# Loading each expert's weights once, in 256 KB pieces split where they land, in a sorted expert MLP kernel

## The reference, cut to what matters

```python
Wi_b, Wo_b = Wi[expert_idx], Wo[expert_idx]            # 512 x 2048 and 2048 x 512 per token
h = gelu(einsum('bsh,bhi->bsi', x, Wi_b) + bi_b)       # 128 x 2048
o = einsum('bsi,bih->bsh', h, Wo_b) + bo_b             # 128 x 512
r = o + x
y = (r - mean(r)) * rsqrt(var(r) + 1e-12) * gamma_b + beta_b
out = rotate(y, theta, phi)
```

## Time and profile before

| | before |
|---|---|
| median of three runs | 2757.75 us (2749.0 to 2760.32) |
| the profiled execution | 2766.84 us, span 2765.0 us |
| TensorE matmul, busy | 2677.4 us (97%) |
| VectorE busy | 1956.6 us (71%) |
| GpSimd busy | 1319.9 us (48%) |
| ScalarE busy | 936.3 us (34%) |
| DMA, mean | 136 GB/s |

### The profile page before, as it was taken

How to read it: one execution, slowest core, us unless ns; L and a number is a source line. 1 busy time by engine, 2 the same in 40 slices (tenths; PEclk the granted TensorE clock), 3 DMA queues, 4 the chain that set the end, 5 groups by cost and what they waited for, 6 DMA issues and landing times.

```text
span 2765.0 us, 54858 instructions
## 1 busy us (share of the span) xinstructions
PE 2677.4 (97%) x12310; PEld 1208.9 (44%) x12311; DVE 1956.6 (71%) x4931; ACT 936.3 (34%) x1697; POOL 1319.9 (48%) x1560
## 2 busy tenths in 40 slices
PE   5999999999999999999999999999999999999998
PEld 2444444444444444444444444444444444444443
DVE  5677777676777776776777776767767776677776
ACT  6333333333333333333333333333333333333332
POOL 0687447860037870677500577607873677500000
PEclk9999999999999999999999999999999999999999
DMA  6766655855455855668644658646665657444343
GB/s 187 187 152 153 154 149 129 182 136 103 87 133 135 184 133 114 170 122 178 140 91 90 159 120 184 144 92 167 166 157 128 172 121 179 111 97 87 83 96 65
DMA packets 741351, 375.98 MB, mean 136 GB/s; under 512 B 682816, under 2 KB 682944, under 8 KB 732608
## 3 DMA queue, kind: packets, MB, share of 16 engines
q1 hardware_dynamic: 677136, 173.16, 35.9%
q0 software_dynamic: 27312, 135.28, 15.2%
q10 hardware_dynamic: 36864, 67.13, 7.9%
HBM read 174.13 MB, written 33.55 MB: 75 GB/s over the span
## 4 chain that ended last, share of the span: by engine, by line
PE 81%; DMA 6%; DVE 5%; issue 4%; DVEq 2%; ACT 2%; ACTq 0%; SPq 0%; POOLq 0%; POOL 0%
PE z_ps L833 41%; PE o_ps L842 40%; DMA xT<-x 3%; DMA xbuf<-in_x 2%; DVE z_ps L641 1%; DMA hT<-h 1%; DVEq L197 1%; ACT z_ps L444 1%; DVE h L651 0%; ACT x L439 0%; DMA wi<-in_L_cond_Wi 0%; ACTq L197 0%; DVE y L696 0%; DVE ln L668 0%; DVE r_ps L667 0%
## 5 line engine op out<-in xcount | busy, mean ns | idle before, releaser
L833 PE MATMUL z_ps<-wi,xT 128*128 x6096 | 1406.5, 381 | 32.3 <-issue 16.1
L842 PE MATMUL o_ps<-wo,hT 128*128 (+1 forms) x6144 | 1410.7, 379 | 10.8 <-DMA hT<-h 10.8
L833 PEld LDWEIGHTS z_ps<-wi,xT 128*128 128x128 f16 x6096 | 598.0, 98 | 763.1 <-issue 61.2
L842 PEld LDWEIGHTS o_ps<-wo,hT 128*128 128x128 f16 x6144 | 601.8, 98 | 739.8 <-issue 19.8
L444 ACT ACTIVATE z_ps<-z_ps 128x512 f32<-128x512 f32 x512 | 299.5, 585 | 1732.3 <-DVE z_ps L641 1727.9
L641 DVE SCALAR_TENSOR_TENSOR z_ps<-z_ps,tok,bi_all 128x512 f32<-128x512 f32 x512 | 387.2, 757 | 195.2 <-PE z_ps L833 133.1
L378 POOL TENSOR_TENSOR wi<-staged 128x512 f32<-128x512 f32 x112 | 118.5, 1058 | 658.1 <-DVE r_ps L661 647.0
L651 DVE SCALAR_TENSOR_TENSOR h<-z_ps,tok,h 128x512 f16<-128x512 f32 x512 | 380.2, 743 | 10.0 <-ACT h L450 9.5
L450 ACT ACTIVATE h<-z_ps,tok 128x512 f16<-128x512 f32 x512 | 351.9, 687 | 19.0
L646 DVE SCALAR_TENSOR_TENSOR x<-xbuf,tok,x 128x512 f16<-128x512 f16 (+1 forms) x128 | 117.2, 916 | 185.8 <-ACT x L439 185.8
L696 DVE SCALAR_TENSOR_TENSOR y<-r_ps,rot,y 128x128 f32<-128x128 f32 x512 | 194.5, 454 | 5.2 <-ACT y L457 2.0
(11 more groups left out here) (126 smaller groups left out, 1366.9 us busy)
## 6 DMA issues: line engine op xcount, KB each, us to landing
staged<-in_L_cond_Wi POOLq DMA_DIRECT2D x56, 1024.0 KB, 5.9
staged<-in_L_cond_Wo POOLq DMA_DIRECT2D x56, 1024.0 KB, 6.6
xbuf<-in_x ACTq DMA_DIRECT2D x128, 256.0 KB, 3.3
out<-y ACTq DMA_DIRECT2D x128, 256.0 KB, 3.4
hT<-h SPq DMA_TRANSPOSE x512, 4.1
bi_all<-in_L_cond_bi POOLq DMA_DIRECT2D x7, 1024.0 KB, 8.3
wi<-in_L_cond_Wi SPq DMA_DIRECT2D x4, 1024.0 KB, 8.5
wo<-in_L_cond_Wo POOLq DMA_DIRECT2D x4, 1024.0 KB, 5.9
```

The lines of the kernel that those rows point to most:

```text
L833: last = t.matmul(z_ps[:, n, :], xT16[:, j, a, k, :], wi16[:, bass.ds(b, 1), w, k, cs], start=(k == 0 and (a, w) == PASSES[0]), stop=(k == ...
L842: last = t.matmul(o_ps[:, j, :], hT16[:, n, a, c, :], wo16[:, bass.ds(b, 1), w, n * GC + c, :], start=(n == 0 and c == 0 and (a, w) == PAS ...
```

## The change

Each expert's weights are loaded once, in 32 pieces of 128 x 512 float32 (256 KB) instead of 16 loads of 1 MB. A piece lands in the place of its own two halves: `wi16` and `wo16` are laid out by piece (`[P, 2, NC, 2, BANK]` with NC = 16 pieces, high half beside low half), so that the 2 KB of a piece in each partition are exactly the float32 piece before the split. `staged` is gone; three small buffers hold a scaled piece, a squared piece and the sum.

Nothing of a rank is loaded ahead of the wait on `s_res` any more. After it, four pieces are issued one behind the other; then each of the 16 steps of Wi waits for its piece, squares it, adds it to the sum and issues the piece four ahead. After every second step comes an eighth of the bias (`bi_piece`, 128 KB). While the 16 pieces of Wi are split, the first 12 steps also wait for a piece of Wo and issue the one four ahead. bo, gamma and beta come one by one in steps 0, 4 and 8 of Wo (256 KB each, `bgb_piece`). The fold starts at 256 columns in place of 1024. The split scales the piece into `scaled`, copies it to the high half and subtracts for the low half. The matmuls read the same 512 columns from new addresses; rank 0 writes its halves through `half_of`.

```diff
-        wi16 = sb("wi16", [P, 2, 2, KH, I], F16)
-        wo16 = sb("wo16", [P, 2, 2, KI, H], F16)
-        staged = sb("staged", [P, 2, QN])
+        wi16 = sb("wi16", [P, 2, NC, 2, BANK], F16)
+        wo16 = sb("wo16", [P, 2, NC, 2, BANK], F16)
+        scaled = sb("scaled", [P, BANK])
+        squared = sb("squared", [P, BANK])
+        summed = sb("summed", [P, BANK])
...
+        def bi_piece(queue, e, b, j, landed):
+            c = slice(j * BIP, (j + 1) * BIP)
+            queue.dma_start(bi_all[:, b, c], bi[bass.ds(e, 1), c].broadcast_to([P, BIP])).then_inc(landed, 16)
+
+        def bgb_piece(queue, e, b, j, landed):
+            v = (bo, gamma, beta)[j]
+            queue.dma_start(bgb_all[:, b, j, :], v[bass.ds(e, 1), :].broadcast_to([P, H])).then_inc(landed, 16)
...
             def split(hi, lo, raw, scale):
-                chain.step(g.tensor_scalar(hi, raw, scale, 1.0, ALU.mult, ALU.mult))
-                chain.step(g.tensor_scalar(raw, raw, scale, 1.0, ALU.mult, ALU.mult))
-                chain.step(g.tensor_tensor(lo, raw, hi, ALU.subtract))
+                chain.step(g.tensor_scalar(scaled[:], raw, scale, 1.0, ALU.mult, ALU.mult))
+                chain.step(g.tensor_copy(hi, scaled[:]))
+                chain.step(g.tensor_tensor(lo, scaled[:], hi, ALU.subtract))
...
-                stage(0)
-                stage(1)
...
+                def load(j):
+                    m, c = divmod(j, NC)
+                    k, n = divmod(c, NB)
                     if m == 0:
+                        source = Wi[bass.ds(e, 1), k * P:(k + 1) * P, n * BANK:(n + 1) * BANK]
                     else:
+                        source = Wo[bass.ds(e, 1), c * P:(c + 1) * P, :]
+                    pool.dma_start(raw(m, c), source.rearrange("e p n -> p (e n)")).then_inc(s_stage[j % 4], 16)
...
+                if not boot:
+                    pool.wait_ge(s_res, before)
+                for j in range(4):
+                    load(j)
+                for c in range(NC):
+                    landed(c)
+                    sum_squares(0, c)
+                    load(c + 4)
+                    if c % 2:
+                        bi_piece(pool, e, b, c // 2, s_bias[b])
+                matrix_scale(0)
+                bias_scale()
+                for c in range(NC):
+                    halves(0, c)
+                    if c < NC - 4:
+                        landed(NC + c)
+                        load(NC + c + 4)
+                g.engine_nop().then_inc(s_wi, 1)
+                if not boot:
+                    pool.wait_ge(s_ln, before)
+                for c in range(NC):
+                    if c >= NC - 4:
+                        landed(NC + c)
+                    sum_squares(1, c)
+                    if c % 4 == 0 and c < 12:
+                        bgb_piece(pool, e, b, c // 4, s_bgb[b])
+                matrix_scale(1)
+                for c in range(NC):
+                    halves(1, c)
+                pool.wait_ge(s_bgb[b], (r + 1) // 2 * 48)
+                g.engine_nop().then_inc(s_wo, 1)
...
-                        last = t.matmul(z_ps[:, n, :], xT16[:, j, a, k, :], wi16[:, bass.ds(b, 1), w, k, cs],
+                        last = t.matmul(z_ps[:, n, :], xT16[:, j, a, k, :], wi16[:, bass.ds(b, 1), k * NB + n, w, :],
```

More of the change, by code:

```diff
@@ L75, in expert_mlp_rotate_kernel @@
     QN = H * I // P // Q
+    NC = H * I // P // BANK
+    CQ = NC // Q
+    BIP = I // (NC // 2)
     XB = 5
@@ L169, in expert_mlp_rotate_kernel @@
         s_bbgb = sem("s_bbgb")
-        s_stage = [sem(f"s_stage{i}") for i in range(2)]
+        s_stage = [sem(f"s_stage{i}") for i in range(4)]
         s_wi = sem("s_wi")
@@ L240, in _ @@
             e0 = slot_value(sp, EXPERT, 0, E - 1)
-            raw = wi16[:, 1].rearrange("p a k n -> p (a k n)").bitcast(F32)
+            raw = wi16[:, 1].rearrange("p c a n -> p (c a n)").bitcast(F32)
             for q in range(Q):
@@ L346, in stage @@
                     else:
[L347 to L355, removed]
-                stage(0)
-                stage(1)
[L359 to L388, removed]
-                    scales(("wi", "wo")[m], pool_s[:, 0:1], b, chain)
[L390 to L404, removed]
@@ new lines, in load, with landed, sum_squares @@
+                        source = Wo[bass.ds(e, 1), c * P:(c + 1) * P, :]
+                    pool.dma_start(raw(m, c), source.rearrange("e p n -> p (e n)")).then_inc(s_stage[j % 4], 16)
+                def landed(j):
+                    pool.wait_ge(s_stage[j % 4], ((r - 1) * 2 * NC // 4 + j // 4 + 1) * 16)
+                def sum_squares(m, c):
+                    to = squared if c else summed
+                    chain.step(g.tensor_tensor(to[:], raw(m, c), raw(m, c), ALU.mult))
+                    if c:
+                        chain.step(g.tensor_tensor(summed[:], summed[:], squared[:], ALU.add))
@@ new lines, in matrix_scale, with bias_scale @@
+                def matrix_scale(m):
+                    fold(summed, BANK)
+                    chain.step(g.partition_all_reduce(pool_s[:, 0:1], summed[:, 0:1], P, ADD_LANES))
+                    scales(("wi", "wo")[m], pool_s[:, 0:1], b, chain)
+                def bias_scale():
+                    pool.wait_ge(s_bias[b], (r + 1) // 2 * 16 * (NC // 2))
+                    for n in range(NB):
+                        piece = bi_all[:, b, n * BANK:(n + 1) * BANK]
+                        chain.step(g.tensor_tensor((squared if n else summed)[:], piece, piece, ALU.mult))
+                        if n:
+                            chain.step(g.tensor_tensor(summed[:], summed[:], squared[:], ALU.add))
+                    scales("bi", fold(summed, BANK), b, chain)
@@ new lines, in halves @@
+                def halves(m, c):
+                    w = (wi16, wo16)[m]
+                    split(w[:, b, c, 0, :], w[:, b, c, 1, :], raw(m, c), wscale[:, m:m + 1])
+                if not boot:
[8 more added lines that the diff above has]
+                        bi_piece(pool, e, b, c // 2, s_bias[b])
@@ L491, in iteration @@
                     sum_x(s + 2, k)
-            raws = [w[:, 1].rearrange("p a k n -> p (a k n)").bitcast(F32) for w in (wi16, wo16)]
-            his = [w[:, 0, 0].rearrange("p k n -> p (k n)") for w in (wi16, wo16)]
-            drop = his[1].bitcast(F32)[:, 0:QN]
+            raws = [w[:, 1].rearrange("p c a n -> p (c a n)").bitcast(F32) for w in (wi16, wo16)]
+            drop = wo16[:, 0].rearrange("p c a n -> p (c a n)").bitcast(F32)[:, 0:QN]
             def squares(m, q):
@@ L737, in iteration @@
                     rotate(s - 2)
-            raws = [w[:, 1].rearrange("p a k n -> p (a k n)").bitcast(F32) for w in (wi16, wo16)]
-            his = [w[:, 0, 0].rearrange("p k n -> p (k n)") for w in (wi16, wo16)]
-            los = [w[:, 0, 1].rearrange("p k n -> p (k n)") for w in (wi16, wo16)]
+            raws = [w[:, 1].rearrange("p c a n -> p (c a n)").bitcast(F32) for w in (wi16, wo16)]
             def exponent(ss):
@@ L769, in lo_parts @@
                     dve.wait_ge(s_bhi, m * Q + q + 1)
-                    v.scalar_tensor_tensor(out=los[m][:, c], in0=raws[m][:, c], scalar=wscale[:, m:m + 1],
-                                           in1=his[m][:, c], op0=ALU.mult, op1=ALU.subtract).then_inc(s_blo, 1)
+                    v.scalar_tensor_tensor(out=half_of(m, 1, q), in0=raws[m][:, c].rearrange("p (c n) -> p c n", n=BANK), scalar=wscale[:, m:m + 1],
+                                           in1=half_of(m, 0, q), op0=ALU.mult, op1=ALU.subtract).then_inc(s_blo, 1)
             dve.wait_ge(s_sin, 1)
@@ L819, in first_product_by_quarters @@
                     for n in range(NB):
-                        cs = slice(n * BANK, (n + 1) * BANK)
                         for a, w in PASSES:
-                            last = t.matmul(z_ps[:, n, :], xT16[:, 0, a, k, :], wi16[:, 0, w, k, cs],
+                            last = t.matmul(z_ps[:, n, :], xT16[:, 0, a, k, :], wi16[:, 0, k * NB + n, w, :],
                                             start=(k == 0 and (a, w) == PASSES[0]),
@@ L841, in second_product @@
                     for a, w in PASSES:
-                        last = t.matmul(o_ps[:, j, :], hT16[:, n, a, c, :], wo16[:, bass.ds(b, 1), w, n * GC + c, :],
+                        last = t.matmul(o_ps[:, j, :], hT16[:, n, a, c, :], wo16[:, bass.ds(b, 1), n * GC + c, w, :],
                                         start=(n == 0 and c == 0 and (a, w) == PASSES[0]),
```

23 lines of the change are left out of this document (10 added, 13 removed).

## The result

Six runs before have a median of 2759.03 us (2749.0 to 2769.24), six after 2735.80 us (2732.87 to 2738.13). The ratio is 0.9909, with a 95% interval of 0.9887 to 0.9930: 0.9% faster, 23 us. The profiled execution after took 2734.06 us.

A forecast was written before the change was run, and what follows sets the result against it. TensorE, busy 97%, was taken to lose time on transposes behind GpSimd's queued loads: 2766.84 - 40.8 + 5 - 3 = 2728.0 us for the profiled execution; 2719 or 2728 for a median run, taken as 2722, range 2709 to 2749.

The forecast's parts named there:

- Two of the prediction's signs: Signs of being right included 0.217 us per matmul throughout and no window after 90 us with a clock below 1.00.
- The loss of 40.8 us: Pipeline from 90 to 2740 us: what TensorE loses beyond its quiet pace, 40.8 us, its cause removed by the change.
- I take 5 us as what stays: Starts after rank 1, where 1 MB still comes at once: some 1 us each stays, 5 us; ends 0 and 20.
- The start: Rank 1's beginning, 76 to 88 us: 6.8 us lost behind 2 MB; with 1 MB 3 come back, ends 0 and 6.8.
- From the profiled execution to the median: Profiled execution 9.1 us above the median: same loss in a median run gives 2719, a larger loss 2728; taken 2722.
- How much GpSimd has queued at once, not its total: GpSimd's load queue: a transpose waits until the backlog is drained; 10.2 us lost behind 2 MB, 5.1 estimated behind 1 MB.
- The vectors: Loads in Wo: three of 256 KB beside 1 MB quarters; afterwards ten microseconds apart, with nothing else of GpSimd's on the way.
- GpSimd's own time: GpSimd's work per rank: from 239 to 268 us, upper end 286, beside TensorE's work and so costing nothing.
- Half stays: Transposes of the pipeline: with half the bytes, half the stalls remain, 2738 us; chance 0.20.
- Only spread: Loads running through Wi's sum and split: 35 tokens lose 1.2 us each, 42 us, time stays about 2758; chance 0.11.
- The due time of GpSimd: Ranks after a short run: uncovered piece latency makes TensorE wait for `s_wi` or `s_wo`, 2859 us; chance 0.07.
- The rule against it: Loads of 256 KB against 1 MiB or more: 32 pieces would cost 83 us per rank against 70, the sum unchanged.

The follow-up runs named there:

- floor run: The kernel after, but GpSimd does nothing from rank 2 on (no loads, sums or splits): 2726.48 us, ratio 0.9867.
- the doubled bytes: The kernel after, but every piece is loaded a second time into a buffer nobody reads, one 256 KB load per step: 2738.86 us, ratio 0.9914.

## Why the prediction was right, and where it was off

The time, 2735.8, lies in the range (2709 to 2749) and on the forecast side of "faster"; it is 14 us above the 2722 of the forecast and just above the forecast's own case (2709 to 2735). The mechanism, stalls of TensorE behind transposes that GpSimd's loads hold up, is what the trace shows: the waits went from 24.2 us to 4.4, and TensorE's quiet pace did not change. Two of the prediction's signs were missed: one window after 90 us has a clock of 0.92 (1840 to 1860), and there 74 matmuls take 0.270 us each instead of 0.217.

- *The loss of 40.8 us* was read rightly: the profiled execution loses 12.6 us after the change, and with the start that makes the 32.6 us of the span. The 16.1 us of waits without a named event were counted in without a cause; 11.9 of them stand behind late transposes of h.
- *"I take 5 us as what stays"* was the term mis-sized: 12.6 stayed, 7.6 more. The bounds, 0 and 20, held it. The floor run says that about 9 of it are GpSimd's work from rank 2 on. *The start* gave 4.1 instead of 3. Summed up as the prediction did, 2728.0 + 7.6 - 1.1 = 2734.5 for the profiled execution, which took 2734.06.
- *From the profiled execution to the median* the prediction left open whether the 9.1 us above the median were a larger loss. They were: six runs before have a median of 2759.03, those after 2735.80, close to the profiled 2734.06. The difference of medians is 23, that of the profiled executions 33. The value between the two, 2722, should have stood at the upper one, 2728.
- *"How much GpSimd has queued at once, not its total"*: the second half is shown (the doubled bytes cost about 3 us). The first half is only part of it. With 2 MB queued at a rank's start the kernel takes 2740 us in four transfers and 2808 in eight. The estimate that 1 MB delays half as long as 2 MB gives 8.2 us to landing, and 6.9 to 7.3 were measured at five of the starts; that is in part luck, since bytes alone don't set the delay. Nor do the transposes wait until the queue is drained: from 617.5 to 623.5 us, in the stretch that the prediction read, 165 of their packets moved beside 231 of GpSimd's. Eight pieces ahead, expected at 2760 at most by that step, is 44 us slower than before.
- *The vectors* were counted among the parts that remove the loss, without a price of their own. Split beside 1 MB quarters they gain nothing (2768.86); between pieces they are worth 7 to 10 us. Of the earlier trace rows the 7.5 us hold for the loads; the first of the vectors took 5.8.
- *GpSimd's own time*, 268 us, was 260, off TensorE's path as said. The copy that no row showed takes 0.62 us; it was taken as 0.717:

```profile
L334 POOL CAST wi<-scaled 128x512 f16<-128x512 f32 x112 | 69.4, 620 | 7.2
```

- *The rivals.* "Half stays" (2738) is the nearest in time, but the profile lost 70% of its stalls, not half. "Only spread" was wrong in its price, 42 us; the doubled load, whose pieces run on through Wo, is at 2738.86. The due time of GpSimd was never near.
- *The rule against it.* The Trainium skill, "DMA: Bandwidth & Descriptors", section "Rules for kernel authors", asks for 1 MiB or more per DMA where the goal is the most bandwidth. The change went against it and gained; but 256 KB transfers back to back in the kernel before lost 20 us, and 512 KB gave the lowest time of those tried, not clear of 256 KB. The measurement decides, and here it gives no single best size.

## What to carry to other kernels

When a kernel that is far from the DMA engines' limit (here 136 GB/s on average, where 400 were seen) stalls in short gaps, look for the large background loads that were issued just before a small transfer on the critical path, and count how many are on the way at once. Keep them few, issued as their places come free: two and four pieces of 256 KB did equally well here, and eight cost 72 us more. Choose the transfer size by experiment; 512 KB with two ahead had the lowest time. Don't take the name on a wait for its cause: ask whether what it names had long been done. Moving one load by one wait can give most of what a new layout gives, so try that first.

## What the runs showed that was not expected

With eight transfers of 256 KB from GpSimd on the way, the DMA engines are busy throughout and move 86 to 116 GB/s in 6 us windows; with four transfers of 512 KB at the same place 277 to 295. With the eight, a packet of a transpose takes up to 82 ns of an engine, where it takes 22 in a quiet stretch and 20 with the four. Why so many transfers slow each other down was not found. And pieces in place of whole loads can cost as well as gain: 20 us more for the weights of the kernel before, 6 us more for its vectors, while the same cut in the kernel after is part of its gain.
